# Output gates carried in the records, expert biases added while mixing, and one GpSimd instruction for decay and the odd step's product

## The reference, cut to what is computed

```python
q, k, v = silu(xn@Wq), l2_norm(silu(xn@Wk)), xn@Wv          # per head: 16 numbers each
gk = log_sigmoid(xn@Wf1@Wf2);  a = k * -sigmoid(xn@Wgamma) * exp(gk)
for each token t:                                            # S: 16x16 per batch and head
    S = S * exp(gk)[..., None]
    sab = einsum('bhk,bhkv->bhv', a, S)
    S = S + k[..., None] * (sab + v)[..., None, :]
    o = einsum('bhk,bhkv->bhv', q, S)
o = o * sigmoid(xn@Wog1@Wog2)                                # the output gate
s = layernorm(o) * norm_w @ Wo
for e in experts: y += cw[:, e] * (gelu(xn@W1[e] + b1[e]) @ W2[e] + b2[e])   # cw: weights of the top 2
out = x + s * silu(layernorm(y) * gamma + beta)
```

## Time and profile before

| | us |
|---|---|
| median of 3 runs | 1249.84 (1248.97 to 1252.61) |
| the profiled execution, its own time | 1244.15 |
| its span in the trace | 1242.4 |
| VectorE busy | 1160.6 (93%) |
| TensorE busy | 934.6 (75%) |
| GpSimd busy | 811.9 (65%) |
| ScalarE busy | 395.0 (32%) |

### The profile page before, as it was taken

How to read it: one execution, slowest core, us unless ns; L and a number is a source line. 1 busy time by engine, 2 the same in 40 slices (tenths; PEclk the granted TensorE clock), 3 DMA queues, 4 the chain that set the end, 5 groups by cost and what they waited for, 6 DMA issues and landing times.

```text
span 1242.4 us, 17665 instructions
## 1 busy us (share of the span) xinstructions
PE 934.6 (75%) x3773; PEld 682.2 (55%) x3774; DVE 1160.6 (93%) x3502; ACT 395.0 (32%) x1047; POOL 811.9 (65%) x902
## 2 busy tenths in 40 slices
PE   5888887100029999999999999999999923567674
PEld 2343343000018888887778788887777823345452
DVE  3799999999999999999999999999999997989882
ACT  3444444200003333333322222332322303454552
POOL 3666666367744777676677777667777765676753
PEclk9798889555559999999999999999999976687776
DMA  5665655553335666666656666666656417355322
GB/s 165 196 215 170 214 181 179 140 192 105 111 93 154 189 191 195 191 195 192 185 170 194 184 179 180 190 190 195 195 165 190 120 38 201 118 152 156 106 81 68
DMA packets 247252, 202.61 MB, mean 163 GB/s; under 512 B 141425, under 2 KB 225233, under 8 KB 247185
## 3 DMA queue, kind: packets, MB, share of 16 engines
q1 hardware_dynamic: 170146, 82.81, 25.3%
q10 hardware_dynamic: 70224, 100.49, 24.3%
q0 software_dynamic: 6816, 18.69, 4.4%
HBM read 139.42 MB, written 62.54 MB: 163 GB/s over the span
## 4 chain that ended last, share of the span: by engine, by line
DVE 53%; issue 16%; PE 15%; DMA 6%; ACT 4%; POOL 3%; SPq 2%; ACTq 0%; DVEq 0%; POOLq 0%
DVE obh L1163 8%; DVE outer L1203 6%; DVE psB L1189 5%; DVE state L1220 5%; PE psA L956 4%; DVE psB L1211 4%; DVE ubuf L1189 4%; PE psF L900 3%; DVE prod_a L1180 3%; DVE ubuf L1191 3%; DMA rec_d<-work 3%; DVE prod_q L1214 3%; PE psF L918 3%; PE psA L888 2%; DVE psB L1199 2%
## 5 line engine op out<-in xcount | busy, mean ns | idle before, releaser
L900 PE MATMUL psF<-wts,work 128*128 128x256 f32 x1248 | 287.6, 383 | 3.2 <-ACT work L709 2.4
L888 PE MATMUL psA<-xgT,wts 128*128 128x256 f32 x1248 | 284.0, 385 | 3.1 <-ACT work L709 2.3
L307 POOL TENSOR_TENSOR decayed<-state,rbh 128x256 f32<-128x256 f32 x200 | 145.5, 727 | 198.3 <-DVE state L1220 177.1
L888 PEld LDWEIGHTS psA<-xgT,wts 128*128 128x128 f32 x1248 | 235.1, 191 | 49.2 <-issue 13.8
L900 PEld LDWEIGHTS psF<-wts,work 128*128 128x128 f32 x1248 | 230.9, 190 | 47.1 <-issue 14.2
L324 POOL TENSOR_TENSOR prod_q<-state,rbh 128x512 f32<-128x512 f32 x175 | 222.8, 1273 | 0.0
L1163 DVE TENSOR_REDUCE obh<-prod_q 128x16 f32<-128x272 f32 x512 | 217.1, 425 | 0.0
L709 ACT ACTIVATE work<-psA,b_sb 128x256 f32<-128x256 f32 x312 | 130.4, 470 | 166.5 <-PE psA L888 158.8
L1180 DVE TENSOR_TENSOR prod_a<-state,psT 128x512 f32<-128x512 f32 x200 | 137.1, 685 | 5.8
L720 ACT ACTIVATE work<-psF,work 128x256 f32<-128x256 f32 x78 | 36.9, 473 | 255.2 <-PE psF L902 252.6
L876 PE MATMUL psT<-ident,work 128*128 128x128 f32 x156 | 24.2, 278 | 120.1 <-DMA work<-xs_d 120.0
(11 more groups left out here) (172 smaller groups left out, 1551.3 us busy)
## 6 DMA issues: line engine op xcount, KB each, us to landing
wts<-in_L_ffn_W_dram ACTq DMA_DIRECT2D x78, 1024.0 KB
rec_d<-work SPq DMA_DIRECT2D x32, 640.0 KB
rbh<-rec_d SPq DMA_DIRECT2D x32, 640.0 KB, 4.5
xs_d<-zero SPq DMA_DIRECT2D x26, 387.0 KB, 8.8
work<-xs_d ACTq DMA_DIRECT2D x39, 258.0 KB
wts<-y_d ACTq DMA_DIRECT2D x16, 512.0 KB, 5.5
x_acc<-in_L_attn_x_dram SPq DMA_DIRECT2D x32, 128.0 KB
og_d<-work SPq DMA_DIRECT2D x32, 128.0 KB, 7.8
```

Source lines behind the costliest of these rows:

```text
L307: eng.tensor_tensor(decayed[:, :, :], state[:, g % SR, :, :], over_v(rbh[:, u, 2 * n, F_:F_ + HD]), ALU.mult).then_inc(s_dec, 1)
L888: mm = pe.matmul(psA[m // 2 % 2][:, m % 2 * MT:(m % 2 + 1) * MT], w1_sb[v][:, c, m * P:(m + 1) * P], xgT[:, c, :], start=(c == 0), stop=(c ...
L900: pe.matmul(psF[q][:, 0:D], hT[:, m, q * P:(q + 1) * P], w2_sb[v][:, m, :], start=(m == 0), stop=False)
```

## The change

- The record grows from 80 to 96 numbers: the output gate is its new part `O_`, next to the decay f. One ScalarE sigmoid of 512 elements writes both. `og_d`, its DMAs and `gate_o` are gone. `gate_outputs` multiplies a whole chunk's outputs (256 elements) before they are stored, at pair 3 of the next chunk (`GATED`): on VectorE up to chunk 7, on GpSimd after that. The stores and loads of SyncE wait for it.
- The matmul with b2 leaves the expert tile. The routing makes a table of expert weights per token, TensorE turns it (`cwT`, 32 rows for 4 tiles), and `add_experts` begins each tile's sum with a matmul of 32 contraction rows.
- In the shared and woven stages a pair has its own function, `two_shared_steps`. GpSimd's `decay_and_read` makes, in one instruction of 512 elements, the decayed state and the product with the odd step's row a. VectorE's first instruction has 256 elements instead of 512.
- `prepared_rows` copies v first and then only half of the rows a. `LAND_STEP` and `PAIR_STEP` are new numbers.

```diff
-REC = 5 * HD
-A_, F_, K_, Q_, V_ = (HD * n for n in range(5))
+REC = 6 * HD
+A_, F_, O_, K_, Q_, V_ = (HD * n for n in range(6))
+GATED = 3
-LAND0, LAND_STEP = 390.0, 16.46
-PAIR_STEP = 3.83
+LAND0, LAND_STEP = 390.0, 14.7
+PAIR_STEP = 3.7
...
+        def gate_outputs(eng, c):
+            eng.tensor_tensor(obh[:, c % OB, :, :], obh[:, c % OB, :, :], rbh[:, c % RB, :, O_:O_ + HD], ALU.mult)\
+                .then_inc(s_og, 1)
-        def decay(eng, g):
+        def decay_and_read(eng, g):
             n, u = g % NP, g // NP % RB
-            eng.tensor_tensor(decayed[:, :, :], state[:, g % SR, :, :], over_v(rbh[:, u, 2 * n, F_:F_ + HD]),
-                              ALU.mult).then_inc(s_dec, 1)
+            wide = [P, 2, HD, HD]
+            rows = rbh[:, u, 2 * n:2 * n + 2, :].rearrange("p j c -> p (j c)")[:, F_:2 * REC - F_ + 2 * A_]
+            rows = rows.rearrange("p (j c) -> p j c", j=2)[:, :, 0:HD]
+            eng.tensor_tensor(prod_a[:, n, 1:3, :, 0:HD], state[:, g % SR, :, :].unsqueeze(1).broadcast_to(wide),
+                              rows.unsqueeze(2).broadcast_to(wide), ALU.mult).then_inc(s_dec, 1)
...
             def spill(n):
                 u4 = n % RS
-                sp.wait_ge(s_og, n + 1)
-                sp.dma_start(og_d[n], ogs[:, u4, :]).then_inc(s_ogd[u4], 16)
...
-                sp.dma_start(fog[:, n % SL, :], og_d[n]).then_inc(s_fl[n % SL], 16)
...
-                if s % NP == 0:
+                if s % NP == GATED:
                     c = WOVEN + s // NP - 1
-                    sp.wait_ge(s_o, (c + 1) * RING)
+                    sp.wait_ge(s_og, c + 1)
...
-                if 3 <= g % NP < 6 and g // NP + 1 < NCH:
-                    prepare_part(g // NP + 1, g % NP - 3)
+                if g % NP == GATED and g // NP > SHARED:
+                    pool.wait_ge(s_o, g // NP * RING)
+                    gate_outputs(pool, g // NP - 1)
+                if 4 <= g % NP < 7 and g // NP + 1 < NCH:
+                    prepare_part(g // NP + 1, g % NP - 4)
...
-                act.activation(rec[:, u4, :, F_:F_ + HD], heads(psF[u][:, 0:D]), ACT.Sigmoid).then_inc(s_f, 1)
-                act.activation(ogs[:, u4, :], psF[u][:, D:2 * D], ACT.Sigmoid).then_inc(s_og, 1)
+                act.activation(rec[:, u4, :, F_:F_ + 2 * HD].rearrange("p h (s c) -> p s h c", s=2),
+                               psF[u][:, :].rearrange("p (s h c) -> p s h c", s=2, h=H), ACT.Sigmoid).then_inc(s_f, 1)
...
-                    pe.matmul(psF[q][:, 0:D], ones[0:1, :], b2_flat[:, bass.ds(e * D, D)], start=False, stop=True)\
-                        .then_inc(s_y, 1)
...
+                    pe.matmul(total, cwT[:, n // 4, :], b2_sb[:, n % 4, :], start=True, stop=False)
                     for c in range(2):
-                        mm = pe.matmul(sums[j % 2][:, n % 2 * D:(n % 2 + 1) * D], ident[:, :], yab[:, g % YR, c, n % GM, :],
-                                       start=(c == 0), stop=(c == 1))
+                        mm = pe.matmul(total, ident[:, :], yab[:, g % YR, c, n % GM, :], start=False, stop=(c == 1))
...
             def prepared_rows(c, u):
...
-                dve.tensor_copy(home_a, rbh[:, u, :, A_:A_ + HD]).then_inc(s_prep, 1)
-                dve.tensor_copy(prod_a[:, :, :, :, HD].rearrange("p n j v -> p (n j) v"), rbh[:, u, :, V_:V_ + HD])\
-                    .then_inc(s_prep, 1)
+                dve.tensor_copy(prod_a[:, :, 0:3:2, :, HD], tok[:, :, :, V_:V_ + HD]).then_inc(s_prep, 1)
+                dve.tensor_copy(home_a, tok[:, :, 0, A_:A_ + HD]).then_inc(s_prep, 1)
```

## The result

The changed kernel takes 1253.62 us (median of 16 runs, 1251.65 to 1261.29) and the kernel before 1251.07 us (median of 16 on the same chip, 1247.58 to 1252.65). The ratio is 1.0033, with a 95% interval from 1.0020 to 1.0047. So it is slower by about a third of a percent. The ratio goes by all executions and is that of their means; the medians alone are 2.6 us or 0.20% apart. The bound of 0.3% (3.7 us) that the prediction gives for what can be told from no change lies between the two.

A forecast was written before the change was run, and what follows sets the result against it. Bounds: VectorE's recurrence in the shared stage, the TensorE-ScalarE chain in the woven stage. Terms 2.3 - 8.4 - 0.5 - 10.1 + 18.5 + 0.2 = +2.0 us on 1244.15 gave 1246.2, raised 0.46% to 1252 us; range 1228 to 1271.

The forecast's parts named there:

- The front: Before the shared pairs: seven VectorE gates of 0.33 us, +2.3 us; bigger records and the rest 0, between -1.5 and +1.5.
- The pair on VectorE: Shared stage: halving the first product shortens each pair from 3.70 to 3.54 us, -26.8 us over 168 pairs.
- The chunk's start: Shared stage: copying v before GpSimd starts cuts new state to next product from 1.73 to 1.19 us, -11.3 us.
- Rival 5: Chunk starts: the copy of v loses to GpSimd's longer instruction, 1.4 us each, 1280 us; chance 0.05.
- GpSimd late: Shared stage: GpSimd's 512-element product makes VectorE wait 0.71 and 0.82 us at pairs 5 and 6, +29.7 us in all.
- Rival 2: Shared stage: GpSimd isn't late, the waits vanish, about -30 us, 1222 us; chance 0.12.
- Shared stage: Recurrence in sum: shorter pairs -26.8, chunk starts -11.3, late GpSimd +29.7, together -8.4 us.
- Start of the woven stage: From pair 224 to the first out_rows: the `og_d` wait goes, 28.0 to 17.9 us, -10.1 us.
- The mixing: Woven-stage rounds: two added 32-row matmuls on the chain, 1.42 us a round, +18.5 us over 13 rounds.
- Rival 3: Mixing: by the page's price for 32 rows, 0.28 us less for each of 26 matmuls, 1245 us; chance 0.06.
- rival 4: Mixing: the added matmuls run at 1.2 GHz, 1.42 us each, +18.5 us, 1270 us; chance 0.14.
- rival 1: Mixing: more TensorE work keeps the clock at 2.4 GHz, rounds 11.5 instead of 12.85 us, -17 us, 1235 us; chance 0.15.

The follow-up runs named there:

- before_rec6: The kernel before with records of six column groups instead of five, the sixth an unread hole of zeros: 1255.98 us against 1247.32.
- all3: The changed kernel with biases of two tiles in TensorE's gap, GpSimd's preparing instructions at pairs 2, 6, 7, and zero fills of xs last: 1198.42 us.
- old_pair: The changed kernel with the shared pair put back as it was before, the rest of the change kept: 1254.91 us.
- copy_order: The changed kernel with the two copies at a chunk's start in the old order, rows a first, v second: 1274.45 us.
- spread: The changed kernel with GpSimd's three preparing instructions of a chunk at pairs 2, 6 and 7 instead of 4, 5 and 6: 1230.21 us.
- filler: The kernel before plus an unused 32-row, 512-column matmul behind turn_y in TensorE's gap, in 14 mixing rounds: 1238.03 us against 1249.03.
- hide: The changed kernel with two tiles' biases in one 32-row, 512-column matmul right behind turn_y in TensorE's gap, out of add_experts: 1226.56 us.
- before_zeros: The kernel before with SyncE's zero fills of xs moved from the front's first tiles to its last: 1246.16 us against 1249.03.

## Why the prediction was right, and where it was not

The forecast was 1252 us, with 1228 to 1271 around it, and 1253.6 came out. By its own bound of 0.3% "slower" (0.35) is what happened if the ratio is taken, and "same" (0.23) if the medians are. "Faster" had the larger chance with 0.42 and did not come. The sum itself was 1246.2 us for the profiled execution, which took 1253.3: 7.1 us too low. The factor 1.0046, by which I raised it to a median, then brought 5.7 us that the changed kernel does not have, since its own profiled execution lies on its median. Two errors of nearly the same size cancelled. That the figure came out within 2 us is luck; most of the mechanisms below came out as described.

- **The front: mis-sized.** +2.3 us was for the gates; "bigger records" and the rest were put at 0, between -1.5 and +1.5. The step that failed is "the loads are chunks ahead". The later loads are, but the write of a record frees the slot that a later tile needs. That wait is 5.3 us (before_rec6: 5.28 us with the bytes alone), and it comes from SyncE's list, on which each of the first records must land before the next is written. The front cost +6.2 us, out of the bounds that I gave. The price of the gates alone is near the forecast: without the wait, in all3, pair 56 is at 386.9 us, against 384.8 to 386.3 in the kernels with before's records. I priced the instructions and not the bytes.
- **The pair on VectorE: right.** 3.56 us for 3.54, so -0.14 us a pair or -23.5 us, for -26.8.
- **The chunk's start: right in its mechanism.** The copy of v takes 0.38 us, the start 1.26 us for 1.19: 0.47 us less than before for the 0.54 forecast, 21 times. Of this the order alone brought 0.35 a start, 7.3 us (old_pair). With the new pair more hangs on the order, 22.7 us (copy_order). Rival 5, the copy that loses to the longer instruction, did not come in the changed kernel. copy_order shows it: 1.02 us a chunk start, where the rival said 1.4.
- **GpSimd late: right, a little too dear.** Pairs 5 and 6, as named, with 0.50 and 0.73 us of wait for 0.71 and 0.82: 1.23 a chunk for 1.53. Rival 2, that GpSimd isn't late, falls. Yet the price of this lateness could have been avoided by other places of three small instructions (spread, -23.4 us), which the prediction did not look for.
- **Shared stage, in sum.** -6.4 us for -8.9. The short pair and the lateness cancel: the stage is 0.7 us longer than that of old_pair. What is left is the order of the copies, 7.2 us (old_pair against before).
- **Start of the woven stage: right in its mechanism, another engine last.** The `og_d` wait is gone, 19.75 us for 17.9 and 28.0 before. I counted VectorE's fourth pair as the last to arrive. The chain that ended last goes through TensorE instead, whose add_experts takes there 6.3 us and not 3.4, at half the pace:

```profile
1045.12 1.15 PE psF L929 x2
1046.27 2.01 PE psF L931 x4
1048.27 1.15 PE psF L929 x2
1049.42 2.02 PE psF L931 x4
```

- **The mixing: right in its sum, not in its parts.** +1.39 us a round for 1.42. The 1.42 was two insertions of 0.71. In the chain an add_experts takes 3.38 us for 1.74 when before's was short: 0.82 us for each insertion. The term was mis-sized at rows 7, where the group behind the insertion lasts 3.72 us and the one ahead of it 3.62, and the prediction counted only the distance between their starts. Against before's long group, 2.59 to 2.80 us, it is only +0.6 to +0.8. Over the twelve rounds, from start to start, the two L929 cost 1.25 us and turn_back 0.12 more than before. The sums behind the biases cost 0.03 less, because they run at full pace in every round, where before's did so in eight of twelve. The rest is 0.05.
- **Rival 3, a lower price for 32 rows, falls, though the page's rule doesn't.** By the Trainium skill, TensorE: Matmul & The Clock Gate, section "Why this matters for your kernels", a single 32-row matmul takes the time of one with 128, and four halves in two insertions would be 0.87 us. On the chain 1.64 us were added. Here are the weight loads (PEld) and matmuls in before, then at the same place in the changed kernel:

```profile
1090.07 1.70 PEld L918 LDWEIGHTS psF<-wts,ident 128*128 128x128 f32 x8
1090.29 1.89 PE L918 MATMUL psF<-wts,ident 128*128 128x256 f32 x8
```

```profile
1125.52 0.73 PEld L931 LDWEIGHTS psF<-wts,ident 128*128 128x128 f32 x4 [0.33 <-issue]
1125.52 1.13 PE L931 MATMUL psF<-wts,ident 128*128 128x256 f32 x4
1126.58 0.29 PEld L929 LDWEIGHTS psF<-b_sb,w_kq 32*128 32x128 f32 x2 [0.33 <-issue]
1126.58 0.69 PE L929 MATMUL psF<-b_sb,w_kq 32*128 32x256 f32 x2
```

In before the first load starts 0.22 us ahead of its matmul. At each change between 128 and 32 rows it starts with it. In the records of the single halves those inside a group are 0.216 us apart. The last half ahead of a change takes 0.30 to 0.31 us and the first behind it 0.32 us, whichever of the two has 32 rows. An add_experts has four changes, at 0.78 us together, and four halves more, 0.86 us: that is the 1.64 us. So the surplus over the page's rule belongs to the changes. What a 32-row half takes between two others of 32 rows no run shows.

- **The clock, rivals 1 and 4.** Neither came. The added matmuls did not run at 1.2 GHz, as rival 4 has it: with them every add_experts from 1060 us on runs at full pace, and the mean granted clock of the twelve rounds rose from 0.76 to 0.80. That is the direction of rival 1, but the rounds did not fall to 11.5 us: the higher clock gives back less than the matmuls cost, and the transposes of turn_back, behind the unchanged gap of 2.70 us, took 391 ns each on average, and 340 ns before. The same work pays when it fills that gap (filler and hide).

## What to carry to other kernels

When an instruction moves to an engine that has time to spare on average, look for the step at which that engine is at its fullest, and move its small work away from there: here that was worth 23 us, and the moved instruction nothing without it. Work that an engine needs anyway costs least in a gap that it sits idle in, and on TensorE here it even gave back more than it cost. A larger transfer is priced by the slot that it frees and by what stands behind it on the issuing engine's list, not only by the data that it brings.

## What the hardware showed that I had not expected

- A matmul that nobody needs made the kernel before 11.0 us faster (filler): the gap ahead of turn_back went from 2.69 to 1.64 us idle, and the mean of one out_rows product from 614 to 559 ns.
- VectorE's copy took 1.49 us when GpSimd's 1.28 us instruction had started 0.03 us before it, and 0.38 us when it started 0.16 us ahead of it. Over 21 chunks the order of two lines is worth 22.7 us.
- Each change between matmuls of 128 and 32 rows cost about 0.2 us, half of it ahead of the change and half behind, and the matmul with one row in the expert tile of before (L902) shows the same steps. Two 32-row matmuls set among 128-row ones thus took 1.64 us.
- The mixing of before falls, for most of its length, into rounds of 11.2 and 12.7 us by turns (before_zeros, before_rec6). That of the changed kernel goes by fours: two rounds of 12.2 us, then 13.3 and 13.5. With the gap filled they are 10.2 to 11.8 (filler).
